# Attention and mixture kernel: project the raw x, loaded turned from DRAM, with column-centred weights, and apply 1/std as the products leave PSUM

## The reference

```
xn = (x - mean(x)) / sqrt(var(x) + 1e-5)           # over the 512 features
x  = x + attn(xn) + ffn(xn)
# attn: proj = xn @ W_in.T -> x-part, z, B, C, dt_low;  dt = softplus(dt_low @ dt_W.T + b)
#   chunks of 64 tokens: masked scores (C.B * decay * dt) @ xp, plus carried states
#   y = y + xp * D;  y = y / rms(y) * norm_w * silu(z);  out = y @ W_out.T
# ffn:  logits = xn @ Wc + bc + tie; in each group of 32 tokens the largest logit picks
#   the token of each of 128 experts; relu(picked @ W1 + b1) @ W2 + b2 goes back to it
```

## Time and profile before

| quantity | value |
|---|---|
| median of 3 runs (range) | 3099.94 us (3097.74 to 3107.66) |
| the profiled execution: its time / its span | 3095.55 us / 3093.6 us |
| PE busy | 2935.3 us, 95% |
| DVE busy | 2470.0 us, 80% |
| ACT busy | 1591.2 us, 51% |
| POOL busy | 1291.7 us, 42% |
| moved by DMA | 286.95 MB, mean 93 GB/s |
| granted TensorE clock, mean | 0.989 of full speed |

### The profile page before, as it was taken

One profiled execution on the slowest core, in us unless ns is written; L12 is line 12 of the kernel. 1 busy time (PEld: TensorE's weight loads), 2 busy tenths in 40 slices (PEclk: granted clock), 3 DMA queues, 4 the chain that ended last, 5 costly groups with the idle time before them and its releaser, 6 DMA issues.

```text
span 3093.6 us, 134808 instructions
## 1 busy us (share of the span) xinstructions
PE 2935.3 (95%) x59784; PEld 2514.9 (81%) x59784; DVE 2470.0 (80%) x3674; ACT 1591.2 (51%) x3614; POOL 1291.7 (42%) x2029
## 2 busy tenths in 40 slices
PE   6999999999999999999999999997888878999999
PEld 5888888888888888888888888886676667888887
DVE  5899899998998998999898999986444447777775
ACT  4555555555555555555555555553333333555555
POOL 3565565655655655656556656553000001000000
PEclk9999999999999999999999999998999999999999
DMA  3221111111111111111111111114444345777765
GB/s 115 70 65 48 57 52 50 54 52 56 55 45 56 55 45 59 52 48 56 52 54 50 52 56 55 45 46 167 142 118 121 107 119 174 228 216 230 226 203 158
DMA packets 336547, 286.95 MB, mean 93 GB/s; under 512 B 52304, under 2 KB 265808, under 8 KB 335072
## 3 DMA queue, kind: packets, MB, share of 16 engines
q1 hardware_dynamic: 335392, 278.16, 29.8%
q10 hardware_dynamic: 576, 0.17, 0.0%
...
## 4 chain that ended last, share of the span: by engine, by line
PE 77%; DVE 15%; issue 5%; DMA 2%; POOL 1%; SPq 1%; DVEq 0%; ACT 0%; POOLq 0%; ACTq 0%
PE a_proj L811 31%; PE s_rt L1479 8%; PE a_mix L811 7%; PE g_pick_ps L1225 5%; PE a_scan L931 4%; PE s_w_ps L1449 4%; PE s_rt L1492 4%; DVE scan_in L673 4%; DVE xs L691 4%; DVE g_picked L1192 3%; PE a_scan L908 2%; PE g_acc_ps L1246 2%; PE a_scan L895 2%; PE a_mix L819 2%; PE a_mix L883 2%
## 5 line engine op out<-in xcount | busy, mean ns | idle before, releaser
L691 DVE TENSOR_SCALAR xs<-gs,mg 64x128 f32<-64x128 f32 x960 | 596.2, 680 | 8.8
L811 PE MATMUL a_proj<-wdh,xnTh 128*128 128x512 f32 x1024 | 419.5, 410 | 0.4 <-DVE wdl L627 0.4
L1428 DVE TENSOR_TENSOR s_resT<-s_w_ps,s_b 128x1024 f32<-128x1024 f32 x252 | 296.9, 1220 | 140.2 <-PE s_w_ps L1449 140.2
L1415 ACT COPY s_res<-s_rt 128x512 f32<-128x512 f32 x512 | 263.1, 600 | 278.1 <-PE s_rt L1479 278.1
L811 PE MATMUL a_proj<-wdh,xnTl 128*128 128x512 f32 x1024 | 402.8, 393 | 0.0
L811 PE MATMUL a_proj<-wdl,xnTh 128*128 128x512 f32 x1024 | 400.8, 391 | 0.0
L673 DVE COPY_PREDICATED scan_in<-mask,a_scan 64x512 f32<-64x512 uint32 x512 | 377.2, 737 | 16.0
L382 POOL TENSOR_TENSOR yv<-yt,dx 128x512 f32<-128x512 f32 x128 | 166.4, 1300 | 439.2 <-DVE yt L699 439.2
L374 POOL TENSOR_TENSOR dx<-xs,d_row 64x512 f32<-64x512 f32 x256 | 328.8, 1285 | 15.1
L1192 DVE COPY g_picked<-g_pick_ps 128x1024 f32<-128x1024 f32 x128 | 156.8, 1225 | 220.7 <-PE g_pick_ps L1225 220.7
L540 ACT ACTIVATE scan_in<-CT,hsel 64x128 f32<-64x128 f32 x1024 | 325.8, 387 | 4.8
...
## 6 DMA issues: line engine op xcount, KB each, us to landing
x<-in_x_dram SPq DMA_DIRECT2D x128, 256.0 KB, 3.2
xn_dram<-xn SPq DMA_DIRECT2D x128, 256.0 KB, 2.3
part_dram<-res SPq DMA_DIRECT2D x128, 256.0 KB, 2.8
g_xn<-xn_dram SPq DMA_DIRECT2D x128, 256.0 KB, 2.9
s_w<-in_w_dram SPq DMA_DIRECT2D x128, 256.0 KB, 4.1
s_part<-part_dram SPq DMA_DIRECT2D x128, 256.0 KB, 3.6
out_dram<-s_out SPq DMA_DIRECT2D x128, 256.0 KB, 2.9
...
```

The lines of the kernel that those rows point to most:

```text
L691: nc.vector.tensor_scalar(dst, gs[rows_, q, :].unsqueeze(1).to_broadcast([CH, 2, 2 * HD]), scale0[rows_, q, :], scale1[rows_, q, :], ALU.m ...
L811: last = nc.tensor.matmul(out, lhs[a], rhs[c], start=(k == 0 and n == 0), stop=(k == nk - 1 and n == 2))
L1415: nc.scalar.copy(res[:, n % 4, :, :], rt_bank[:, n % 3, :, :]).then_inc(res_cp, 1)
L1428: last = nc.vector.tensor_tensor(resT[m % 2][j][:, :, sets].rearrange("p n (q r) -> p n q r", r=4), w2_place(u)[:, :, :, j * GB:(j + 1) * ...
```

## The change

DRAM gets a second copy of x, laid out turned (`xT`: block, 128 features, 4 x 256). SP loads one block of it per step into `xr` (512 KB), two steps ahead; block 0 goes into the buffer of `yz`. ACT writes h of the whole block (`hi_x`, 128 x 1024), DVE l (`lo_x`, 128 x 1024, both inputs in SBUF). PE's `transpose_xn` is gone.

Since the projected x is raw, the weights lose their column means at the start: PE multiplies the staged weights by a matrix of 1/512 (`column_means`, plain fp32) and DVE subtracts the result (`centre`). The mean of x then drops out. 1/std of a token is applied where the products are read: as a scale of ACT's copies (B and dt, x, silu of z), in `scale_y` (C), and, for the logits, where tokens lie along the row, by a product with `rsb`. `rsb` is 1/std written to DRAM (`store_rs`, 256 pieces of 4 bytes) and read back to all partitions (`load_rsb`). The normalised `xn`, still needed by the expert phase, is written by ACT (`normalize`) instead of DVE, with a bias that POOL makes in two more small instructions. The first of the expert weights `w1`, whose place `xr` takes, is loaded at step 64 instead of step 4.

```diff
+    def xr_place(s):
+        return xr[:, s % 2, :, :] if s > 0 else yz[:].rearrange("p i (k t) -> p (i k) t", t=ST)
...
+        def load_xr(s):
+            sync.dma_start(xr_place(s), io["xT"][s]).then_inc(xr_in[s % 2], 16)
...
+        def store_rs(s):
+            sync.wait_ge(ln_pool, 4 * (2 * s + 1) + 2)
+            sync.dma_start(rs_cols[s], rs[:, 2 * s:2 * s + 2], allow_slow_non_contiguous=True).then_inc(rs_out, 16)
+        def load_rsb(s):
+            sync.wait_ge(rs_out, 16 * (s + 1))
+            wait(sync, pm, 4 * (s - 2) + 1)
+            sync.dma_start(rsb[:, s % 2, :], rs_rows[s].partition_broadcast(P)).then_inc(rsb_in[s % 2], 16)
...
+                load_xr(0)
+                sync.dma_start(x[:, 2, :], x_dram[2]).then_inc(x_in[2], 16)
                 for t in range(2):
                     store_xn(t, t)
+                store_rs(0)
...
+        load_rsb(0)
+        sync.wait_ge(w_lo, LAST_STAGE)
+        load_xr(1)
...
         for s in range(NST + 2):
-            if s == STB:
-                sync.wait_ge(w_lo, len(stages))
-                gather["load_w1"](sync, 0)
             if s == NST:
                 sync.wait_ge(lg_ps, NST)
+                gather["load_w1"](sync, 0)
                 gather["load_first"](sync)
...
             for i in range(2):
+                if i == 0 and valid(s + 2):
+                    sync.wait_ge(xT_lo, s + 1)
+                    load_xr(s + 2)
+                if valid(s + 1):
+                    (store_rs, load_rsb)[i](s + 1)
                 if valid(s + 1 + i):
                     store_xn(2 * (s + 1 + i) + 1 - i, 1 - i)
...
             nc.gpsimd.tensor_tensor(ve[:, j:j + 1], mv[:, j, 1:2], ln_eps[:], ALU.add).then_inc(ln_pool, 1)
-            pool.wait_ge(ln_pool, 2 * n + 1)
-            nc.gpsimd.tensor_tensor(mv[:, j, 1:2], ve[:, j:j + 1], mhalf[:], ALU.pow).then_inc(ln_pool, 1)
+            pool.wait_ge(ln_pool, 4 * n + 1)
+            nc.gpsimd.tensor_tensor(rs[:, n:n + 1], ve[:, j:j + 1], mhalf[:], ALU.pow).then_inc(ln_pool, 1)
+            nc.gpsimd.tensor_scalar(nm[:, j:j + 1], mv[:, j, 0:1], -1.0, 1.0, ALU.mult, ALU.mult).then_inc(ln_pool, 1)
+            pool.wait_ge(ln_pool, 4 * n + 3)
+            nc.gpsimd.tensor_tensor(nb[:, j:j + 1], nm[:, j:j + 1], rs[:, n:n + 1], ALU.mult).then_inc(ln_pool, 1)
...
+        def hi_x(s):
+            act.wait_ge(xr_in[s % 2], 16 * (s // 2 + 1))
+            wait(act, lg_ps, s - 1)
+            nc.scalar.copy(xT[s % 2][0][:], xr_place(s)).then_inc(xT_hi, 1)
...
+        def normalize(n):
+            act.wait_ge(ln_pool, 4 * n + 4)
+            wait(act, xn_out[n % 2], 16 * (n // 2))
+            nc.scalar.activation(xn[:, n % 2, :], x[:, n % (2 * STB), :], ACT.Identity, bias=nb[:, n % 2:n % 2 + 1],
+                                 scale=rs[:, n:n + 1]).then_inc(xn_ready, 1)
...
+            if n < LAST_STAGE:
+                act.wait_ge(centred, n + 1)
...
+                hi_x(0)
+                for t in range(2):
+                    normalize(t)
...
+            nc.scalar.activation(raw[:, n % 4, :], proj[n % 2][:, 0:C_C], ACT.Copy, scale=rs[:, n:n + 1]).then_inc(bdt_cp, 1)
...
             if valid(s + 1):
-                hi_xn(2 * (s + 1), 1 - par, 0)
-            if valid(s):
-                copy_bdt(n0 + 1)
+                hi_x(s + 1)
...
+            if valid(s + 1):
+                normalize(2 * (s + 1) + 1)
...
+            if valid(s + 2):
+                normalize(2 * (s + 2))
...
+        def lo_x(s):
+            dve.wait_ge(xT_hi, s + 1)
+            nc.vector.tensor_tensor(xT[s % 2][1][:], xr_place(s), xT[s % 2][0][:].bitcast(F32), ALU.subtract).then_inc(xT_lo, 1)
...
+        def centre(n):
+            dve.wait_ge(mean_ps, 1 + n // 2)
+            view, banks = stage_view(n), scan_bank[:, n // 2 * 2:n // 2 * 2 + 2, :].rearrange("p b c -> p (b c)")
+            cols = view.shape[2]
+            for c0 in range(0, cols, 512):
+                c1 = min(c0 + 512, cols)
+                last = nc.vector.tensor_tensor(view[:, :, c0:c1], view[:, :, c0:c1],
+                                               banks[:, c0:c1].unsqueeze(1).to_broadcast([P, 2, c1 - c0]), ALU.subtract)
+            last.then_inc(centred, 1)
...
+            dve.wait_ge(ln_pool, 4 * n + 2)
+            nc.vector.scalar_tensor_tensor(yt[:].rearrange("p (b h d) -> p b h d", b=2, h=H // 2),
+                                           scan_bank[:, 2:4, HALF:512].rearrange("p b (h d) -> p b h d", h=H // 2),
+                                           rs[:, n:n + 1], gain, ALU.mult, ALU.mult).then_inc(yt_cp, 1)
...
+            dve.wait_ge(rsb_in[s % 2], 16 * (s // 2 + 1))
...
+            nc.vector.tensor_tensor(lg[:], proj[1][:, 0:ST], rsb[:, s % 2, :], ALU.mult).then_inc(pm, 1)
+            dve.wait_ge(pm, 4 * s + 1)
+            nc.vector.scalar_tensor_tensor(view, view, bc_col[:], tie_row[:].unsqueeze(1).to_broadcast([P, groups, GRP]),
+                                           ALU.add, ALU.add).then_inc(pm, 1)
...
+        dve.wait_ge(dt_in, 32)
+        nc.vector.tensor_reduce(wsum[:], wlow[:], AX_X, ALU.add).then_inc(dt_mean, 1)
+        dve.wait_ge(dt_mean, 1)
+        nc.vector.tensor_scalar(wmean[:], wsum[:], 1.0 / D, 1.0, ALU.mult, ALU.mult).then_inc(dt_mean, 1)
+        dve.wait_ge(dt_mean, 2)
+        nc.vector.tensor_scalar(wlow[:], wlow[:], wmean[:], 1.0, ALU.subtract, ALU.mult).then_inc(dt_mean, 1)
...
+            if n % 2 == 0:
+                centre(n)
+                centre(n + 1)
...
+                lo_x(0)
...
                 scale_y(n2 + 1)
-            if valid(s + 1):
-                lo_xn(2 * (s + 1), 1 - par, 0)
...
             if valid(s + 1):
+                lo_x(s + 1)
                 stats(2 * (s + 1) + 1)
                 finish_stats(2 * (s + 1) + 1)
-                normalize(2 * (s + 1) + 1)
...
                 scale_y(n1)
-            if valid(s + 1):
-                lo_xn(2 * (s + 1) + 1, 1 - par, 1)
...
-            if valid(s + 2):
-                normalize(2 * (s + 2))
...
-        def transpose_xn(n, j):
-            pe.wait_ge(xn_ready, n + 1)
-            wait(pe, xnT_lo, n)
-            wait(pe, res_cp, n - 6)
-            for k in range(KD):
-                last = nc.tensor.transpose(mix[:, k * P:(k + 1) * P], xn[:, j, k * P:(k + 1) * P], ident[:])
-            last.then_inc(xnT_ps, 1)
...
-            pe.wait_ge(xnT_lo, mixed)
...
+        def column_means(n):
+            view = [stage_view(n + i) for i in range(2)]
+            cols = view[0].shape[2]
+            pe.wait_ge(zeroed, 4)
+            for i in range(2):
+                pe.wait_ge(w_in[i], 16 * (n // 2 + 1))
+            for b, c0 in enumerate(range(0, cols, 512)):
+                c1 = min(c0 + 512, cols)
+                for k in range(KD):
+                    last = nc.tensor.matmul(scan_bank[:, n + b, 0:c1 - c0], mean[:], view[k // 2][:, k % 2, c0:c1],
+                                            start=(k == 0), stop=(k == KD - 1))
+            last.then_inc(mean_ps, 1)
...
+        pe.wait_ge(dt_mean, 3)
...
-        for i in range(2):
-            transpose_xn(i, i)
+        column_means(0)
+        pe.wait_ge(const_in, NCONST)
...
-                wait(pe, xnT_lo, n0 + 2)
+                pe.wait_ge(xT_lo, s + 1)
                 project_bdt(n0)
-            if valid(s + 1):
-                transpose_xn(n0 + 2, 0)
-            if valid(s):
                 project_bdt(n0 + 1)
+            if s == 0:
+                column_means(2)
...
-            if valid(s + 1):
-                transpose_xn(n0 + 3, 1)
...
+        xT=L0_attn_x.reshape(NST, ST, KD, P).transpose(0, 3, 2, 1),
```

More of the change, by code:

```diff
@@ L137, in attention_phase @@
     xn = sb("xn", [P, 2, D])
-    xnT = [[sb(f"xnT{n}{b}", [P, KD, ST], F32R, at=AT_XNT + 4096 * (2 * b + i)) for i, n in enumerate("hl")] for b in range(2)]
+    xr = sb("xr", [P, 2, KD, ST], at=AT_W1 + 8192)
+    nm = sb("nm", [P, 2])
+    nb = sb("nb", [P, 2])
+    rs = sb("rs", [P, NT])
+    rsb = sb("rsb", [P, 2, ST])
+    mean = sb("mean", [P, P])
+    wsum = sb("wsum", [R, 1])
+    wmean = sb("wmean", [R, 1])
+    xT = [[sb(f"xT{n}{b}", [P, KD, ST], F32R, at=AT_XNT + 4096 * (2 * b + i)) for i, n in enumerate("hl")] for b in range(2)]
     raw = sb("raw", [P, 4, C_C])
@@ L189, in attention_phase @@
     xn_ready = sem("xn_ready")
-    xnT_ps = sem("xnT_ps")
-    xnT_hi = sem("xnT_hi")
-    xnT_lo = sem("xnT_lo")
+    dt_in = sem("dt_in")
+    dt_mean = sem("dt_mean")
+    mean_ps = sem("mean_ps")
+    centred = sem("centred")
+    xr_in = [sem(f"xr_in{i}") for i in range(2)]
+    xT_hi = sem("xT_hi")
+    xT_lo = sem("xT_lo")
+    rs_out = sem("rs_out")
+    rsb_in = [sem(f"rsb_in{i}") for i in range(2)]
     bdt_ps = sem("bdt_ps")
@@ L300, in store_xn @@
             sync.dma_start(xn_dram[n], xn[:, j, :].rearrange("p (k c) -> p k c", k=KD)).then_inc(xn_out[j], 16)
-        for t in range(3):
+        def load_xr(s):
[8 more added lines that the diff above has]
```

(30 more changed lines are left out.)

63 lines of the change are left out of this document (24 added, 39 removed).

## The result

| | us |
|---|---|
| before, median of 4 runs (3097.74 to 3107.66) | 3101.57 |
| after, median of 4 runs (3270.60 to 3299.56) | 3283.80 |
| after / before, 95% interval | 1.0588 [1.0536, 1.0639] |
| after, profiled execution; its span | 3270.60; 3268.5 |

The account below looks back on a forecast made before the run. PE was taken as the first bound with DVE right behind. From 3095.55 us, 50.4 off for 63 steps plus 21.5 for the start gave 3066.7, forecast as a median of 3070; own range 3054 to 3087, wider range 3038 to 3112.

Parts of the forecast that it names:

- The step of PE and DVE: Steady step, attention phase: 0.80 us off 32.70, giving 31.90 us, PE at 31.94 and DVE at 31.9.
- yz's wait for yv: DVE, both halves of a step: about 1.2 us waiting for POOL's yv, with cexp right behind yt.
- the removed xnTl: DVE behind yt: xnTl only filled the wait for POOL's yv; removal saves 0.07 us each, 0.14 per step.
- the wait for x: DVE's wait for x from DRAM, 0.76 us per step: about half filled by lo_x ahead of the statistics.
- PE's own term: PE, steady step: eight transposes go, 0.76 us per step, making PE's step 31.94 us.
- what lies beside: Other engines and queues: small additions on ACT and POOL; SP's three more issues per step put at nothing.
- The start: Before the first step: column means, centring and later weight loads cost +21.5 us, bounds 15 and 30.
- M: Start: time when PE's column means of w_tok are done, taken as 17.5 us; later start times count from it.
- PE's wait for the dA of step 0: Start: PE's later wait of 2.32 us goes, since its chain runs under the longer start.
- a lock of DVE and POOL: Rival: POOL's long instructions meet lo_x or yz, 1.28 us waited per step; 33.2 us steps, 3153 us, chance 0.14.
- The meeting of cexp and yv: DVE and POOL: cexp, two SBUF inputs, took 1.39 us beside yv; a warning that lo_x is exposed, unpriced.
- The other two rivals: DVE gives only 0.45 us per step, 3093 us, chance 0.18; or 1.1 per step, short start, 3048, chance 0.16.

Follow-up runs that it names:

- e8_row_in_sbuf: The change with 1/std's 4-byte pieces written to a row in SBUF, which goes to DRAM as 1 KB; ratio 0.9938 to the kernel before.
- e1_no_trip: The change without store and spreading load of 1/std after step 0, logits scaled by step 0's row; 3077.37 us, ratio 0.9960 to the kernel before.
- e3_load_only: The change without the 1/std store after step 0, the spreading load kept, always of row 0; 3083.52 us, ratio 0.9982 to the kernel before.
- f12_start: The change with 1/std's row built in SBUF, raw weights loaded straight to their low parts' places, start reordered; 3046.83 us, ratio 0.9847 to the kernel before.

## Why the prediction was wrong, point by point

**The step of PE and DVE was right.** Without the harm in it, e8_row_in_sbuf takes (2081.8 - 72.9) / 63 = 31.89 us per step (e1_no_trip 31.84, e3_load_only 31.87); the forecast was 31.90:

```profile
L679 ACT COPY mg<-a_misc x64: 185/185/186, 72.9 to 2081.8; 128x32 f32<-128x32 f32 x64
...
PE a_scan L998 <- DVE scan_in L745: 10.5, 28, 0.5
PE a_proj L887 <- issue: 5.2, 5, 1.9
...
DVE yz L780 <- POOL yv L434: 122.4, 94, 2.3
...
DVE bst L705 <- DMA x<-in_x_dram: 6.8, 10, 2.0
```

The terms, from this run: yz's wait for yv is 1.30 us per tile (forecast 1.2), and from yt to yz it is 2.52 us in the median without xnTl and was 2.53 with it in the kernel before, so the removed xnTl really was only a filling; the wait for x fell from 0.76 to 6.8 / 47 = 0.14 per step, more than the half taken; lo_x took 1.23 us (forecast 1.14), the first step of the picks 425 ns (0.43). PE's waits for the masks stayed, 0.22 per step, so PE's own term decided. That it was hit to 0.01 us is partly luck: PE's busy time fell by 0.90 us per step (1484.10 in 45.9 steps before, 1479.48 in 47.0 here) where 0.76 was read for the transposes, and its idle time rose by 0.09.

**The step that failed is a "nothing".** Under what lies beside, the prediction said of SP's three new issues that 1/std goes to DRAM in the first half of a step and is needed at the end of the next, and put down "Nothing for these, up to 3 us for the last". That asks whether somebody waits for the transfer. It does not ask what the transfer does to others. The price is (34.72 - 31.89) x 63 = 178 us. It splits, from the 300 to 1800 us windows of after and of e8_row_in_sbuf:

```profile
300.00:1800.00 1500.00, 1411.86 (x24631) 1196.04 (x24632) 1178.10 (x2028) 865.68 (x2026) 873.73 (x1508) 0.97 0.29 69
```

```profile
300.00:1800.00 1500.00, 1479.48 (x26836) 1262.66 (x26836) 1290.64 (x2208) 943.22 (x2209) 952.80 (x1645) 1.00 0.26 75
```

In 43.2 and 47.0 steps PE is idle 2.04 us per step against 0.44, 1.60 more, and busy 32.68 against 31.45 for the same products, 1.23 more. The second part fits the lower clock: 0.97 instead of 1.00 is 3% of a step, about 1.0 us.

**The start, forecast +21.5 us, was +39.3.** Its first half was good: means until 16.2 (M = 17.5), first projection at 23.72 (25.3), loads of w_dz out at 24.12 (25.5). Then two things. First, the same store stands ahead of these loads. In all twelve runs of the change that keep the 4-byte store of step 0, the change included, the first mg comes at 80.3 to 84.2 us; in e8_row_in_sbuf it comes at 72.9. The DMA view of 20 to 60 us, one GB/s number per microsecond, of after and then of e8_row_in_sbuf:

```profile
GB/s 0 0 0 183 295 171 246 82 16 33 49 16 33 41 82 156 361 410 385 66 0 0 0 0 0 0 0 0 0 0 0 0 0 0 0 0 0 139 377 393
...
stage<-in_w_dz_dram SPq DMA_DIRECT2D x2, 1024.0 KB, 14.6
```

```profile
GB/s 0 0 0 92 285 148 131 279 393 410 451 393 41 0 0 0 0 0 0 0 0 0 0 0 0 0 0 0 0 0 188 303 311 279 331 416 418 369 135 20
...
stage<-in_w_dz_dram SPq DMA_DIRECT2D x2, 1024.0 KB, 6.3
```

For eight microseconds, 27 to 35, all queues together move under 100 GB/s; the loads land after 14.6 us instead of 6.3. No instruction is fetched on q8 or q14 in this window of after: the store holds up other transfers of data too. In e8 the means of w_dz begin at 33.06 (M + 15.5 = 33.0) and `project_x` at 51.60 (51.1) instead of 58.35; the first mg is 8.4 us earlier than in after. Second, the prediction let PE's wait for the dA of step 0 vanish. In e8 it is 6.78 us, since ScalarE stands in front of the softplus in hi_x, waiting for the second turned block, whose load waits in SP's queue for the last low part of w_dz:

```profile
58.78 1.04 ACT L528 CAST xTh<-xr 128x1024 fp32r<-128x1024 f32 x1 [7.99 <-DMA xr<-in_xT_dram]
...
65.61 0.34 PE L1006 MATMUL a_misc<-dA,umat 128*32 128x32 f32 x8 [6.78 <-POOL dA L469]
```

That order was in the diff: `load_xr(1)` behind `wait_ge(w_lo, LAST_STAGE)`, and hi_x ahead of `softplus` on ACT. In f12_start, where the block is loaded early, the wait is 0.62 us. These two leave about 2 of the 18 us open.

**The sum of the miss**, 3283.8 - 3070 = 214 us: the steps 178, the start 18, the part behind the last mg 8 (999.8 against 991.7 us; in the other runs it is 985 to 1004 without a pattern), 9 because after's median lies 13 us above its profiled execution where 4 were assumed, and 1 from rounding 3071.1 to 3070.

**The rivals.** The side "slower" had 0.14, for a lock of DVE and POOL that did not come: in after lo_x is

```profile
L704 DVE TENSOR_TENSOR xTl<-xr,xTh x63: 1224/1226/1241, 69.1 to 2215.3; 128x1024 fp32r<-128x1024 f32 x63
```

1241 ns at most. The Trainium skill, in "SBUF — State Buffer", section "Who interferes with whom", would allow a block there, since lo_x has two inputs in SBUF; no run here shows one at lo_x. The meeting of cexp and yv that the prediction took its warning from did change sides. Before, and then after:

```profile
L659 DVE TENSOR_TENSOR cexp<-CT,hsel x128: 681/1262/1412, 51.5 to 2125.8; 128x512 f32<-128x512 f32 x128
L382 POOL TENSOR_TENSOR yv<-yt,dx x128: 1259/1289/1660, 66.3 to 2138.6; 128x512 f32<-128x512 f32 x128
```

```profile
L722 DVE TENSOR_TENSOR cexp<-CT,hsel x128: 678/681/871, 89.1 to 2292.9; 128x512 f32<-128x512 f32 x128
L425 POOL TENSOR_TENSOR yv<-yt,dx x128: 1261/1662/1732, 106.9 to 2306.4; 128x512 f32<-128x512 f32 x128
```

Without xnTl between them cexp starts first and keeps its 0.68 us, and yv is the longer one; since yz needs both, nothing was won or lost by it. The other two rivals were variants of the gain. All four cases put the added DMAs at nothing. That the DMA engines are 18% busy would not have helped: a busy share says nothing of a stretch in which little is moved and everything is late. The prediction's own tests did point at the miss ("if the step is above 32.3 us"), and PE's waits for "issue" at its place.
